# A GRU behind a causal convolution: x of the later steps in 256-byte runs, Toeplitz blocks asked for by GpSimd

## The reference

```
x: (128, 64, 512) f32    cond: (128, 512) f32    (batch 128, 64 steps, 512 channels; taps K = 128)
x = x + causal_depthwise_conv1d(x, w=cond[:, None, :]) + b        # left pad K-1, over the 64 steps
# GRU over the 64 steps, h0 = cond, x_t = x[:, t, :]
gi = x_t @ W_ih + b_ih ;  gh = h @ W_hh + b_hh                    # (512, 1536) each
r = sigmoid(i_r + h_r) ;  z = sigmoid(i_z + h_z) ;  n = tanh(i_n + r * h_n)
h = (1 - z) * n + z * h
out[:, t, :] = x_t + h
```

## Time and profile before

| | |
|---|---|
| time, median of 3 runs | 1238.42 us |
| profiled execution, its own time | 1239.42 us |
| its span, first to last instruction | 1237.5 us |
| mean granted TensorE clock | 0.991 |
| PE busy | 1182.9 us, 96% of the span |
| PE weight loads busy | 986.4 us, 80% |
| DVE busy / ACT busy / POOL busy | 539.3 / 500.2 / 17.2 us |
| DMA, mean over the span | 79 GB/s; 150 to 183 GB/s from 60 to 370 us |

### The profile page before, as it was taken

How to read it: one execution, slowest core, us unless ns; L and a number is a source line. 1 busy time by engine, 2 the same in 40 slices (tenths; PEclk the granted TensorE clock), 3 DMA queues, 4 the chain that set the end, 5 groups by cost and what they waited for, 6 DMA issues and landing times.

```text
span 1237.5 us, 15341 instructions
## 1 busy us (share of the span) xinstructions
PE 1182.9 (96%) x5518; PEld 986.4 (80%) x5518; DVE 539.3 (44%) x811; ACT 500.2 (40%) x934; POOL 17.2 (1%) x19
## 2 busy tenths in 40 slices
PE   1997999899989999999999999999999999999997
PEld 1976788787878888888888888888888888888886
DVE  2835766476655333333333333333333333333333
ACT  4436766576755333323333323333332333332332
POOL 0400000000000000000000000000000000000000
PEclk9999999899989999999999999999999999999999
DMA  9978888788853111111011111001111101111100
GB/s 244 293 176 161 167 173 175 170 183 174 173 149 77 54 32 35 34 34 32 24 29 34 34 34 34 25 25 34 34 34 34 28 24 34 34 34 34 32 17 21
DMA packets 288354, 97.98 MB, mean 79 GB/s; under 512 B 212752, under 2 KB 282384, under 8 KB 286272
## 3 DMA queue, kind: packets, MB, share of 16 engines
q1 hardware_dynamic: 283968, 96.29, 33.1%
q10 hardware_dynamic: 4352, 1.25, 0.4%
HBM read 63.34 MB, written 34.14 MB: 79 GB/s over the span
## 4 chain that ended last, share of the span: by engine, by line
PE 89%; ACT 3%; issue 2%; SPq 2%; DMA 2%; DVE 2%; ACTq 0%; DVEq 0%
PE bank L779 80%; PE bank L801 4%; PE bank L741 2%; PE bank L768 2%; SPq L347 1%; ACT tmp L561 1%; ACT x_parts L551 1%; SPq L358 1%; DMA early<-early_result 1%; ACT bank L519 0%; ACT toep_early L500 0%; DMA xres<-stage 0%; DVE stage L679 0%; DVE x_parts L668 0%; DMA tap_pad<-tap_rows 0%
## 5 line engine op out<-in xcount | busy, mean ns | idle before, releaser
L779 PE MATMUL bank<-w_ih_hi,xT_hi 128*128 128x512 f32 x768 | 308.2, 401 | 0.0
L779 PE MATMUL bank<-w_ih_hi,xT_lo 128*128 128x512 f32 x768 | 302.2, 394 | 0.0
L779 PE MATMUL bank<-w_ih_lo,xT_hi 128*128 128x512 f32 x768 | 302.2, 393 | 0.0
L779 PE MATMUL bank<-w_hh_hi,hT_hi 128*128 128x512 f32 x768 | 299.6, 390 | 0.0
L779 PE MATMUL bank<-w_hh_lo,hT_hi 128*128 128x512 f32 x768 | 299.5, 390 | 0.0
L779 PE MATMUL bank<-w_hh_hi,hT_lo 128*128 128x512 f32 x768 | 298.8, 389 | 0.0
L779 PEld LDWEIGHTS bank<-w_ih_hi,xT_lo 128*128 128x128 f32 x768 | 145.6, 190 | 31.8
L779 PEld LDWEIGHTS bank<-w_hh_hi,hT_lo 128*128 128x128 f32 x768 | 144.2, 188 | 30.4
L779 PEld LDWEIGHTS bank<-w_ih_hi,xT_hi 128*128 128x128 f32 x768 | 146.1, 190 | 27.2 <-ACT bank L519 0.4
L779 PEld LDWEIGHTS bank<-w_ih_lo,xT_hi 128*128 128x128 f32 x768 | 146.1, 190 | 26.8
L779 PEld LDWEIGHTS bank<-w_hh_hi,hT_hi 128*128 128x128 f32 x768 | 144.4, 188 | 28.1
(11 more groups left out here) (59 smaller groups left out, 802.3 us busy)
## 6 DMA issues: line engine op xcount, KB each, us to landing
x_unit<-in_x_dram SPq DMA_DIRECT2D x64, 256.0 KB, 4.7
toep_ring<-kernel_parts SPq DMA_DIRECT2D x128, 128.0 KB, 3.3
out_dram<-outZ SPq DMA_DIRECT2D x256, 64.0 KB, 1.6
xres<-stage SPq DMA_DIRECT2D x32, 384.0 KB, 5.0
xT<-xres SPq DMA_DIRECT2D x192, 64.0 KB, 1.9
early<-early_result SPq DMA_DIRECT2D x4, 1024.0 KB, 13.8
xT<-early SPq DMA_DIRECT2D x60, 64.0 KB, 2.0
w_ih_raw<-in_L_cond_W_ih_dram SPq DMA_DIRECT2D x12, 256.0 KB, 7.8
```

The source lines that it names most:

```text
L779: mm = nc.tensor.matmul(psum[:, :], a[:, rows], b[w][:, cols], start=False, stop=stop and n == 2, skip_group_check=True)
```

## The change

- x of the later steps: units are 64 pairs (4 MB), and a run is 64 floats, 256 bytes. A unit lies in two halves (64 of the 128 batch rows each, 2 MB, four DMAs) in a ring `x_ring` of three halves; HALF_OF says which two slots a unit takes. Unit 0 and the second half of unit 1 are asked for at the start, the other half of a unit once the unit before it is split, and the first half of the unit after soon behind it. Splits of the first three blocks of a unit stand later (one to three banks ahead, not four).
- Toeplitz blocks: POOL issues all 128 DMAs, four blocks at once and then each when the block four before it has been used.
- Stages are 8 pairs (a store every 4 banks). There is one outZ, and outT is the tile q; DVE waits for outZ of the step before ahead of its first write of q, and for the stores of the step before ahead of the transpose.
- At the start, ACT does x_row_by_k first and k_full, hT_hi, k_parts ahead of the issues of bias_d and bias_pair; PE waits for y0 only ahead of the bank that it lies in. SP asks for unit 0 without a wait for toep_cleared and k_parts_stored.

```diff
-    UNIT = 32
+    UNIT = 64
     NUNIT = PAIRS // UNIT
-    STAGE = 16
+    UNIT_BLOCKS = UNIT // BLOCK
+    HALF = B // 2 * UNIT
+    HALF_OF = ((0, 1), (0, 2), (1, 2), (0, 1))
+    HALF_USE = ((1, 1), (2, 1), (2, 2), (3, 3))
+    STAGE = 8
...
-    x_unit = [place(f"x_unit{n}", B * UNIT) for n in range(2)]
+    x_ring = place("x_ring", 3 * HALF)
...
-            if m is None or m % 2 or m // 2 + 2 >= NBLOCK:
+            if m is None:
                 return None
-            return m // 2 + 2
+            for j in (m // 2 + 2, (m + 3) // 2, (m + 1) // 2):
+                ahead = (1, 2, 3)[j % UNIT_BLOCKS] if j % UNIT_BLOCKS < 3 and j >= UNIT_BLOCKS else 4
+                if 2 * j - ahead == m and j < NBLOCK:
+                    return j
+            return None
...
+            def load_x_half(unit, half):
+                n = HALF_OF[unit][half]
+                for part in range(2):
+                    b0 = half * B // 2 + part * B // 4
+                    for c in range(2):
+                        ch = unit * 2 * UNIT + c * UNIT
+                        cols = slice(n * HALF + part * HALF // 2, n * HALF + (part + 1) * HALF // 2)
+                        sp.dma_start(
+                            x_ring[c * T:(c + 1) * T, cols].rearrange("s (b g) -> s b g", g=UNIT),
+                            x[b0:b0 + B // 4, :, ch:ch + UNIT].rearrange("b s g -> s b g"),
+                        ).then_inc(x_half_loaded[n], 16)
...
-            sp.wait_ge(toep_cleared, 1)
-            sp.wait_ge(k_parts_stored, 16 * QUADS)
-            for b4 in range(4):
-                load_x_quarter(0, b4)
-            for j in range(T_RING):
-                load_toep(j)
+            for half in range(2):
+                load_x_half(0, half)
             load_early_xT(2)
             load_early_xT(3)
-            for b4 in range(4):
-                load_x_quarter(1, b4)
+            load_x_half(1, 1)
...
-                if m % 2 == 0 and m >= 2 and m // 2 + 3 < NBLOCK:
-                    sp.wait_ge(conv_done, m)
-                    load_toep(m // 2 + 3)
-                if m % 8 == 2 and m > 2:
-                    store_stage(m // 8 - 1)
...
+                if m % 4 == 2 and m > 2:
+                    store_stage(m // 4 - 1)
+                unit = (m + 5) // 32
+                if 1 <= unit < NUNIT:
+                    if (m + 5) % 32 == 0:
+                        sp.wait_ge(x_lo_ready, unit * UNIT_BLOCKS)
+                        load_x_half(unit, 0 if unit == 1 else 1)
+                    if (m + 5) % 32 == 3 and unit < NUNIT - 1:
+                        load_x_half(unit + 1, 0)
...
+            def load_toep(j):     # on POOL: pool.dma_start, the access patterns as before
...
+            pool.wait_ge(toep_cleared, 1)
+            pool.wait_ge(k_parts_stored, 16 * QUADS)
+            for j in range(NBLOCK):
+                if j >= T_RING:
+                    pool.wait_ge(conv_done, 2 * (j - T_RING) + 2)
+                load_toep(j)
...
+                if j % UNIT_BLOCKS == 0:
+                    for half in range(2):
+                        act.wait_ge(x_half_loaded[HALF_OF[j // UNIT_BLOCKS][half]],
+                                    16 * 4 * HALF_USE[j // UNIT_BLOCKS][half])
...
+                if isinstance(i, bass.RuntimeValue) or t > 0:
+                    dve.wait_ge(outZ_ready, t)
                 dve.wait_ge(gh_n_done, t + 1)
...
-                if isinstance(i, bass.RuntimeValue) or t >= 2:
-                    dve.wait_ge(out_stored[u % 2], 16 * QUADS * (2 * i + u // 2))
-                nc.vector.transpose(outZ[u % 2][:, :], outT[:, :]).then_inc(outZ_ready, 1)
+                if isinstance(i, bass.RuntimeValue) or t > 0:
+                    dve.wait_ge(out_stored, 16 * QUADS * t)
+                nc.vector.transpose(outZ[:, :], outT[:, :]).then_inc(outZ_ready, 1)
...
-            pe.wait_ge(y0_ready, KB)
...
+                if slot == 0 and conv_bank[n % 3] is ps_x0 and n < 3:
+                    pe.wait_ge(y0_ready, KB)
```

More of the change, by code:

```diff
@@ L107, in conv_residual_gru @@
     stage = [place(f"stage{n}", STAGE * B) for n in range(2)]
-    outT = place("outT", D)
     r, z, n_gate, q = (place(n, D) for n in ("r", "z", "n_gate", "q"))
-    outZ = [place(f"outZ{n}", D) for n in range(2)]
-    xT2, xT3 = place("xT2", D), place("xT3", D)
+    outT = q
+    outZ = place("outZ", D)
+    xT1, xT2, xT3 = place("xT1", D), place("xT2", D), place("xT3", D)
     gru_end = top[0]
-    xT0, xT1 = place("xT0", D), place("xT1", D)
+    xT0 = place("xT0", D)
     xT = [xT0, xT1, xT2, xT3]
@@ L199, in conv_residual_gru @@
         early_stored = [sem(f"early_stored{n}") for n in range(QUARTERS)]
-        x_unit_loaded = [sem(f"x_unit_loaded{n}") for n in range(2)]
+        x_half_loaded = [sem(f"x_half_loaded{n}") for n in range(3)]
         toep_loaded = [sem(f"toep_loaded{n}") for n in range(T_RING)]
@@ L230, in conv_residual_gru @@
         outZ_ready = sem("outZ_ready")
-        out_stored = [sem(f"out_stored{n}") for n in range(2)]
+        out_stored = sem("out_stored")
         ROUNDS = T // RING
@@ L285, in x_block @@
         def x_block(j):
-            c0 = j % (UNIT // BLOCK) * BLOCK
-            unit = j // (UNIT // BLOCK) % 2
-            return x_unit[unit][:, :].rearrange("p (b g) -> p g b", g=UNIT)[:, c0:c0 + BLOCK, :]
+            unit, g0 = j // UNIT_BLOCKS, j % UNIT_BLOCKS * BLOCK
+            first, second = HALF_OF[unit]
+            at = x_ring[:, first * HALF + g0:first * HALF + g0 + BLOCK]
+            return bass.AP(at.tensor, at.offset, [at.ap[0], [1, BLOCK], [(second - first) * HALF, 2], [UNIT, B // 2]])
         def part_block(j, low):
-            return parts[j % HL_RING][:, :].rearrange("p (g l b) -> p g l b", l=2, b=B)[:, :, low, :]
+            return parts[j % HL_RING][:, :].rearrange("p (g l h b) -> p g l h b", l=2, h=2, b=B // 2)[:, :, low]
         block = ctx.enter_context(nc.Block())
@@ L429, in _ @@
             rounds(sp, step)
-            for n in range(2):
-                sp.wait_ge(out_stored[n], 16 * QUADS * T // 2)
+            sp.wait_ge(out_stored, 16 * QUADS * T)
         @block.gpsimd
@@ L458, in _ @@
             nc.gpsimd.memset(toep_ring[:, :].bitcast(F32), 0.0).then_inc(toep_cleared, 1)
+            def load_toep(j):
+                unit, g = j * BLOCK // UNIT, j * BLOCK % UNIT
+                for c in range(2):
+                    ch = unit * 2 * UNIT + c * UNIT + g
+                    first = kernel_parts[ch:ch + BLOCK, :, 0:T]
+                    source = bass.AP(first.tensor, first.offset, [[1, T], [P, 2 * BLOCK], [1, T]])
+                    pool.dma_start(
+                        toep[j % T_RING][c * T:(c + 1) * T].bitcast(F32).rearrange(
+                            "s (n e) -> s n e", e=P)[:, :, c * T:(c + 1) * T],
+                        source,
+                    ).then_inc(toep_loaded[j % T_RING], 16)
+            pool.wait_ge(toep_cleared, 1)
[4 more added lines that the diff above has]
+                load_toep(j)
         @block.scalar
@@ L464, in tap_columns @@
                 return tile[:, :].rearrange("p (k j) -> p k j", j=P)
+            act.wait_ge(x_row_loaded, 16)
+            nc.scalar.activation(x_row_by_k[:, :].rearrange("b (k q r) -> b q k r", k=KB, r=QUAD),
+                                 gate_in_order(x_row), ACT.Copy).then_inc(x_row_by_k_ready, 1)
             act.wait_ge(tap_zeros_set, 1)
@@ L474, in _ @@
                           ).then_inc(tap_blocks_loaded, 16)
+            act.wait_ge(hT_done, 1)
+            act.wait_ge(k_zeroed, 1)
+            nc.scalar.activation(tap_columns(k_full)[:, :, 0:T], tap_columns(ps_hT)[:, :, T:P],
+                                 ACT.Copy).then_inc(k_full_copied, 1)
+            nc.scalar.activation(hT_hi[:, :], ps_hT[:, :], ACT.Copy).then_inc(hT_hi_ready, 1)
+            act.wait_ge(k_full_ready, 1)
+            nc.scalar.activation(k_parts[:, :].rearrange("p (k l j) -> p k l j", l=2, j=P)[:, :, 0, 0:T],
+                                 tap_columns(k_full)[:, :, 0:T], ACT.Copy).then_inc(k_hi_ready, 1)
             for q4 in range(QUADS):
@@ L601, in step @@
                 split(split_block(t, 8))
+                split(split_block(t, 7))
                 first_half(bulk_bank(t, 7))
```

55 lines of the change are left out of this document (12 added, 43 removed).

## The result

The changed kernel takes **1383.47 us** (median of 4 runs, 1381.07 to 1386.49) beside 1240.21 for the kernel before on the same chip: ratio 1.116 (95% interval 1.112 to 1.119), 143 us slower. The forecast was 1334, in a range of 1207 to 1392. The sign and the mechanism came out as forecast; the amount is half as large again (143 us, not 94).

What follows compares the result with a forecast made beforehand. PE, 96% busy, was taken to bound the kernel, losing time to late Toeplitz blocks before 395 us. Sum: 1239.4 us + 94.3 (POOL's DMAs one at a time) + 0 for the other parts = 1334 us, range 1207 to 1392.

Steps and rivals of the forecast that it cites:

- (1) POOL's pace: Toeplitz DMAs on POOL go one at a time, 3.3 us each, shifting the last bank by 94.3 us; chance 0.60.
- The bound of 1398: Upper end of the forecast's own range: Toeplitz DMAs one at a time at a 3.8 us landing, +158 us.
- 60 roughly equal stalls: Sign of being right: PE idle before the banks grows from 22 to about 110 us, in stalls two banks apart.
- The room inside a block for the lower clock: PE's work fits a block's 6.6 us: 4.3 us, or 6.1 with one clock drop of 1.75.
- The first rival: POOL writes next descriptors during a DMA's flight, under 2.16 us each; 1223 us, range 1205 to 1236; chance 0.32.
- The rival "in time": Toeplitz blocks from POOL arrive in time: stalls go, -24.0, new ones +8; 1223 us, 1205 to 1236; chance 0.32.
- the six stalls: PE's "issue" waits at 86 to 395 us in the kernel before, 18.2 us, put down to late Toeplitz blocks.
- (2) x: Later steps' x loads: first bank up to 5 us later, cost 0; if POOL were fast, 1 to 5 us per edge.
- The missing half of a unit: x's 2 MB for later units: 10.4 us to load, asked for at about bank 26, 13.0 us before bank 32.
- second rival: Blocks in time but x takes 17 us, each edge stalling some 7 us; 1241 us, 1232 to 1252; chance 0.08.
- (3) The start order: ACT's early orders: early convolution starts at 25 to 27 us, not 29.95, but hidden; value 0, down to -4.
- (4) Stages of 8: Smaller stages, one outZ: stores asked for a step (16.80 us) before, so no wait; 0, at most a few us.

Runs made afterwards that it cites:

- experiment 1: The changed kernel with dynamic_dma_scratch_size 1088 instead of 1024, 64 bytes more room for POOL's DMA descriptors; 1248.5 us.
- experiment 5: The kernel before with only the Toeplitz DMAs moved from SyncE to POOL, 1024 bytes for descriptors; 1379.00 us, ratio 1.112.
- experiment 6: The kernel before with only the Toeplitz DMAs moved to POOL and 2048 bytes for its descriptors; 1209.76 us, ratio 0.975.
- experiment 2: The changed kernel with dynamic_dma_scratch_size 2048 instead of 1024, twice the descriptor room; 1249.5 us.
- (8): The changed kernel with 1088 bytes of descriptor room, x loads after the start leaving out half the batch rows (output differs); 1233.89 us, ratio 0.994.
- Experiment 9: The kernel before with Toeplitz DMAs on POOL, 2048 bytes of descriptor room, and the change's start order added; 1209.13 us, ratio 0.976.
- experiment 12: The kernel before with Toeplitz DMAs on POOL, 2048 bytes of room, plus stages of 8 pairs, one outZ, outT in q; 1235.37 us, ratio 0.993.
- experiment 10: The kernel before with only the Toeplitz DMAs moved to POOL and 1088 bytes for its descriptors; 1246.17 us, ratio 1.003.

## Why the prediction was right, and where it was off

**(1) POOL's pace: right in kind, mis-sized.** One Toeplitz DMA at a time is what POOL's timeline shows, 64 bytes of room end it (experiment 1), and the part alone, on the old x, gives the whole loss (5). The term was 128 x 3.3 = 422.4 us from the first issue to the last landing, the median landing of before and nothing between two DMAs. It measured 470.9 us (62.1 to 533.0). Two things were wrong in it. The larger one was put at nothing: the step from a landing to the next start, 0.30 us each time and 39.8 us in all, with the one wait for a slot. The smaller one is the size of the landing: a sum goes by the mean, which was 3.37 us (the median 3.1), 431.1 us for 128 and so 8.7 more. Less 2.2 us for the earlier start (62.1, not 64.3), and with 3.0 us where 2.2 was taken from the last landing to the last bank, that is 47.1: the last bank was forecast at 488.9 and came at 536.0.

The pace is not the steady 3 us that was to show it either, but 3.1 us in quiet stretches and 4.2 to 5.6 beside x. The bound of 1398, from the busy landing of 3.8, lay above the measured time partly by luck: the landings were shorter than that, and the 0.30 us took up the difference. PE's idle time at the banks was forecast to grow to about 110 us and grew to 122.5; the "60 roughly equal stalls" are some 50, of up to 5.1 us but for the one at bank 0. The room inside a block for the lower clock was there: the 41 us of slower work lie inside the pace of the DMAs and are not added to it, since the pace alone explains the last bank's shift.

Four sizes on the old x, 1024, 1088, 1536 and 2048 bytes, give 1379.0, 1246.2, 1241.6 and 1209.8 us. In their traces at most one, two, two and three DMAs are under way at once: the time goes by this count, not by the bytes in between. That I took the upper end, one at a time, rested on an estimate of mine of how much room one DMA takes, which no row of before and no run shows; what the runs show are these counts. The first rival had POOL write the next descriptors while the last DMA is in flight. By the traces it does not start a second DMA beside the first at 1024 bytes (never two under way), which is what would have been needed.

**The rival "in time"** holds on the old x with 2048 bytes, where three are under way at the most (6). Its gain was put at up to 24.0 us; experiment 6 has 30.7 (1240.5 before on that chip by its ratio, to 1209.8), 28.3 of them ahead of the last bank. Beside the six stalls it also clears DVE's stage waits at the banks (2.7 us) and the lower clock behind all of them. On the new x it does not hold: experiments 1 and 2 are at 1248.5 and 1249.5, above its range of 1205 to 1236.

**(2) x: wrong at the edges once POOL is fast.** In the change itself it is nearly hidden, as forecast: bank 0 starts at 93.28 us, 6.9 later than 86.43, where 0 to 5 was said, and no edge behind it waits for x. Unit 0 took 24.7 us from 66.21 to its last landing at 90.9, not 20.7. With POOL fast the three later edges cost 5.52, 4.67 and 9.27 us (experiment 1), where I had said 1 to 5. Two terms failed. The missing half of a unit was to take 10.4 us, the pace of x_early; beside Toeplitz blocks and stores it took 14.4, 14.3 and 14.8 us. And it was to be asked for 13.0 us before it is needed, at bank 26; block 15's split ended at 156.89, as bank 27 began, and the half was asked for at 156.92, 11.2 us before the time at which bank 32 would have started. Ahead of bank 96, block 47's split ended at 311.97, but SyncE was still issuing reloads of xT and a stage's store until 315.22, and asked for x at 315.27; 3.3 us of this edge, the longest, come from there. This is the second rival's mechanism, "in time, but x late" at 1241 (1232 to 1252), which I gave 0.08. Experiments 1 and 2 land in its range. Halving the bytes (8) takes some 15 us back.

**(3) The start order: right at 0.** The early convolution begins at 22.93 us, not 29.95, earlier even than the 25 to 27 forecast, and it buys nothing: PE then waits 3.4 us more for the bias in the bank and longer at bank 0. Experiment 9 shows the same without POOL's stalls.

**(4) Stages of 8: right in the change, wrong as a reason.** DVE's wait for the stage's store sums to 1.0 us there. But POOL's slow pace covers it: experiment 12, with fast blocks, has 49.3 us of such waits and costs 25.6 us. The step that failed is "asked for a step before, so in time": I looked at outZ's stores, 16.80 us apart, and not at the stage's, which at half the size come round twice as often and stand in SyncE's queue behind up to 8.65 us of x DMAs.

**What adds up.** From experiment 6 at 1209.8 us to experiment 2 at 1249.5 the new x ring, its order and the stages of 8 cost 39.7 us. The change in POOL's queue costs 1379.0 - 1240 = 139 us with 1024 bytes of room, and gives 30.7 with 2048. With pairs (1088) old and new x are alike, 1246.2 and 1248.5: my reading, which no run isolates, is that the two delays overlap there. How the 39.7 us divide between late x and late stage stores is open. In experiment 2 PE waits 32.0 us for x_parts at the four edges, and DVE 19.7 us for the stage's stores (8 waits of up to 4.4 us), but with the new x SyncE issues x at other moments, and the 25.6 us of experiment 12 were measured with the old.

## What to carry to other kernels

When DMAs are moved to GpSimd, run the move with more than one `dynamic_dma_scratch_size`, and look in its timeline how many stand in a row. Here, one at a time at 1024 bytes, each cost its whole time from issue to landing in turn, 3.37 us on the mean, and 0.30 us more. For a sum take the mean landing under the traffic of that stretch, not the median (here 3.1). The same move was worth -31 us with 2048 bytes and +139 with 1024. A term put at zero because something slower covers it should be written down as "zero while covered": take the cover away, and it is a cost that the fix of the first fault brings out.

## What the runs showed of the hardware

- In these profiles POOL's wait that hangs on the room stands as "issue" time ahead of its DMAs, not as a named wait: 371.9 us in the change, 115.5 us in experiment 1. At 1024 bytes a DMA starts 0.30 us after the landing of the one before (126 of 127 in the change); at 1088 bytes, 0.33 us after the second of the pair has landed (61 of 63 in experiment 10), not after the first.
- Pieces with half the runs take POOL 0.61 to 0.63 us each, a whole DMA 0.69, so cutting each DMA in two nearly doubled POOL's issue time here. In 1024 bytes it was a gain all the same (3 and 1 in a row, 1346.8 against 1383.5 us); beside the pairs of whole DMAs it was a loss (1280.6 at 1152 bytes against 1248.5 at 1088).
- One at a time, the same DMA landed as fast from POOL (the change) as from SyncE: 2.8/3.1/5.3 us (least, median, longest) against 2.7/3.3/5.4. With up to three under way it was slower: 2.8/3.8/6.8 in experiment 6.
- Twice the run length did not make x arrive twice as fast. At the start the change's eight DMAs (4 MB, 256-byte runs) hold SyncE for 19.01 us and have landed after 24.7; in experiment 5, with the same room for POOL, eight DMAs of the old x (2 MB, 128-byte runs) hold it for 13.40 us and have landed after 16.5. A byte took about three quarters of the time, not half.
